# Products of zeros ahead of a conv, and the last tile's products in two halves of the columns

## The chip, the cores and the metric

The kernel runs on one core of one Trainium2 chip. The metric is the device time of one execution in microseconds (us); for the kernel before it is 1641.54 us, the median of three runs (1641.47 to 1641.69).

## The reference, cut to what matters

An input x of 128 sequences, 32 rows each, 512 columns, goes through two blocks, each with a residual:

```python
x = x + attention(conv1d(x) + cond @ c_weight.T + bias)     # grouped conv, 9 taps, 4 groups of 8 rows
x = x + ffn(mix(x, cond))
# mix: att = softmax(gelu(gelu(cond @ W0 + b0) @ W1 + b1) @ W2 + b2); per sequence, a 32x32 matrix
#      att @ weight mixes the 32 rows, and att @ bias_k is added
# ffn: out = x @ base_W.T + low-rank part of the top 2 of 28 experts (rank 8), gated by their softmax
```

The attention has 32 query heads and 8 key heads of 128, with weights given as 4-bit codes and scales.

## The kernel before, in words

The kernel is written engine by engine: each engine has a program of its own, and semaphores (`wait_ge`, `then_inc`) order them. What stands in an engine's program is executed in that order. It has two blocks.

The first block, `prepare_and_convolve`, does the conv, in fp32. SP issues the loads: `params` (which holds cond, W0, W1, W2 and their kin), `band` (the conv taps as a banded matrix), then x in 16 pieces of 512 KB, one for each pair of a 128-column tile k and a group g, in the order in which the conv wants them. TensorE (line 347 on) waits for `params` and runs the small chain that gives the softmax over the 8 matrices: a product into `ctx_psum` for the conv's bias, w0, w1 behind ScalarE's gelu of w0's result, w2 behind the gelu of w1's. VectorE adds the bias and computes the softmax (lines 391 to 403). Behind w2 TensorE goes through the 32 half units of the conv, `conv(n)`: half unit n is 64 of the 128 positions of one unit (k, g), and consists of four products of 160 or 192 columns (line 323) and one or two of 32 columns (lines 328 and 332) that carry the taps over the edge. Results go to banks 0 to 2. VectorE adds the bias into `h_f`, a buffer of two units (`add_ctx`, line 384); `turn(n - 2)` transposes 128x128 pieces of `h_f` on TensorE into banks 3 to 5 (line 344), and ScalarE and VectorE split each into two fp16 parts, high and low, in `hT` (lines 477 and 389). `h_f[:, 1]` is first written by `add_ctx(2)`, and bank 5 by `turn(2)`. An fp32 product shows as two instructions in the profile, and so two of the rows' "x" are one product. The block ends for all engines together when each has finished its program.

The second block, `attention_and_ffn`, goes through 8 key heads and 8 chunks of 512 tokens, with about 90% of the time, and then through 32 tiles of 128 tokens for the mix and the ffn. For a tile t of the steady part, TensorE's order is: `gate_lora(t)` (12 products of 252 columns, line 857: expert logits and low-rank activations of all experts), `mix(t + 1)`, `transpose_acc(t + 3)`, `lora_out(t - 1)` (6 products of 512 columns that close tile t - 1, line 893), `base_out(t)` (12 products of 512 columns into bank 2 or 3, line 872; each accumulation of three passes works on high and low fp16 parts) and `lora_transpose(t)` (line 884), which needs VectorE to have chosen and gated the experts (lines 1162 to 1192). ScalarE and VectorE then take the transposed result out of its bank in two fp16 parts (lines 1508 and 1199), and only then can `lora_out(t)` run. `finish(t)` (line 1206) adds the residual on VectorE and writes `res`, and SP stores it (`store`, line 687), 256 KB for a tile. `y_bank` (bank 0) takes the result of `mix`, and `add_bias` (line 1147) reads it. In the last tile there is no mix and no next tile, so `lora_out(31)` and `finish(31)` follow with nothing beside them.

Of the kernel before, what the change touches and what calls it, by code (L numbers as in the profile page):

```python
# [14 lines left out]
P = 128  # L15
# [140 lines left out]
def prepare_and_convolve(nc, c, a, bank, accT, hT, w, rows):  # L156
# [10 lines left out]
    def sem(name):  # L167
        return c.enter_context(nc.semaphore(name))
# [28 lines left out]
    f_src = sb("f_src", [P, 2, 512])  # L197
    f_hl = sb("f_hl", [P, 2, 2, 512], F16)

    params_loaded = sem("params_loaded")  # L200
    kern_loaded = sem("kern_loaded")
    ident_loaded = sem("ident_loaded")
# [101 lines left out]
    @block.tensor  # L304
    def _(pe):
        def conv(n):

            k, g = unit(n // 2)
            j0 = n % 2 * 4
            if n < 2:  # L310
                pe.wait_ge(band_loaded, 16)
            if n % 2 == 0:
                pe.wait_ge(x_loaded[k][g], 16)
            elif k < KT - 1:
                pe.wait_ge(x_loaded[k + 1][g], 16)
            if n >= 3:
                pe.wait_ge(h_added, n - 2)
            out = bank[n % 3].rearrange("p (s l) -> p s l", s=CG)
            for j in range(4):

                lo, hi = max(LB * j - PAD, 0), min(LB * j - PAD + LT, HALF)
                m0 = lo - (LB * j - PAD)
                pe.matmul(out[:, :, lo:hi], xT[:, k, g, j0 + j], band[:, g, :, m0:m0 + hi - lo], start=j == 0, stop=False,
                          skip_group_check=True)
            mm = None
            if n % 2 or k:
                kk, jj = (k, j0 - 1) if j0 else (k - 1, BLOCKS - 1)
                mm = pe.matmul(out[:, :, 0:PAD], xT[:, kk, g, jj], band[:, g, :, LT - PAD:LT], start=False,
                               stop=n % 2 == 1 and k == KT - 1, skip_group_check=True)
            if n % 2 == 0 or k < KT - 1:  # L330
                kk, jj = (k, j0 + 4) if j0 == 0 else (k + 1, 0)
                mm = pe.matmul(out[:, :, HALF - PAD:HALF], xT[:, kk, g, jj], band[:, g, :, 0:PAD], start=False, stop=True,
                               skip_group_check=True)
            mm.then_inc(conv_psum, 1)

        def turn(t):
            u, half = t // 2, t % 2
            if t == 0:
                pe.wait_ge(ident_loaded, 16)
            pe.wait_ge(h_added, 2 * u + 2)  # L340
            if t >= 3:
                pe.wait_ge(hT_ready, t - 2)
            for s in range(4):
                mm = pe.transpose(bank[3 + t % 3][:, s * P:(s + 1) * P], h_f[:, u % 2, 4 * half + s], w.ident[:])
            mm.then_inc(hT_psum, 1)

        pe.wait_ge(params_loaded, 16)
        pe.matmul(bank[6][:, 0:S], cond_T, cw_T, start=True, stop=True).then_inc(ctx_psum, 1)
        pe.matmul(bank[7][:, 0:B], w0, cond_T, start=True, stop=True).then_inc(hid_psum, 1)
        pe.wait_ge(ctx_added, 1)  # L350
        pe.wait_ge(hid_done, 1)
        pe.matmul(bank[6][:, 0:B], w1, hid[:, 0], start=True, stop=True).then_inc(hid_psum, 1)
        pe.wait_ge(hid_done, 2)
        pe.matmul(bank[7][:, 0:COND_K], hid[:, 1], w2, start=True, stop=True).then_inc(att_psum, 1)
        for n in range(2 * UNITS):
            conv(n)
            if n >= 2:
                turn(n - 2)
            if n == 3:
                pe.wait_ge(att_step, 5)  # L360
                pe.transpose(bank[6][0:COND_K, 0:B], att[:], w.ident[:]).then_inc(att_T_psum, 1)
            if n in (4, 5):
                if n == 4:
                    pe.wait_ge(kern_loaded, 16)
                    pe.wait_ge(att_T_done, 1)
                m = n - 4
                pe.matmul(bank[7 - m], att_T[:], kern[:, 512 * m:512 * (m + 1)], start=True, stop=True).then_inc(agg_psum, 1)
            if n == 6:
                pe.wait_ge(agg_done, 1)
                pe.matmul(bank[7][:, 0:S], att_T[:], kern[:, S * S:], start=True, stop=True).then_inc(agg_psum, 1)  # L370
        turn(2 * UNITS - 2)
        turn(2 * UNITS - 1)

    @block.vector
    def _(dve):
# [59 lines left out]
        def f_lows(m):  # L435
# [3 lines left out]
            dve.scalar_tensor_tensor(out=lo, in0=f_src[parts, m % 2, 0:cols], scalar=FSCALE, in1=hi, op0=ALU.mult,  # L439
                                     op1=ALU.subtract).then_inc(f_low, 1)  # L440

        dve.wait_ge(ctx_psum, 1)
        dve.tensor_tensor(ctx_sb[:], bank[6][:, 0:S], fside, ALU.add).then_inc(ctx_added, 1)
        softmax()
# [54 lines left out]
def attention_and_ffn(nc, c, a, banks, accT, hT, w, rows, out):  # L499
# [144 lines left out]
        return banks[:, 2 + t % 2]  # L644


    def at(step):

        return step[0] * CHUNKS + step[1]
# [16 lines left out]
    def _(sp):  # L666
# [15 lines left out]
        def load_x(t):  # L682
            sp.dma_start(tile_of(t), x_rows[t]).then_inc(x_loaded[t % XTILES], 16)
# [21 lines left out]
        wait_chunk(7)  # L705
        for t in range(XTILES // 2, XTILES):
            load_x(t)
        for t in range(TILES):
            store(t)
            if t + XTILES < TILES:  # L710
                load_x(t + XTILES)
        for n in range(2):
            sp.wait_ge(out_stored[n], 16 * TILES // 2)

    @block.tensor
    def _(pe):
# [116 lines left out]
        def mix(t):  # L833
            if t == 0:
                pe.wait_ge(mixw_loaded, 16 * 2 * TB)
                pe.wait_ge(q_cos_done[0], STEPS)
                pe.wait_ge(q_sin_done[0], STEPS)
            else:
                pe.wait_ge(y_added, t)
            pe.wait_ge(xs_ready, t + 1)  # L840
            for k in range(KT):
                for i, (xp, wp) in enumerate(PASSES):
                    mm = pe.matmul(y_bank[:, k * P:(k + 1) * P], x_hl[:, t % 2, xp, k * P:(k + 1) * P], mixw[:, wp, t],  # L843
                                   start=i == 0, stop=i == 2)
            mm.then_inc(y_psum, 1)
# [16 lines left out]
        def base_out(t):  # L862
            if t >= 2:
                pe.wait_ge(res_done, t - 1)
            else:
                pe.wait_ge(base_loaded, 16)
                pe.wait_ge(q_cos_done[1], STEPS)
                pe.wait_ge(q_sin_done[1], STEPS)
            i = 0
            for k in range(KT):  # L870
                for yp, wp in PASSES:
                    pe.matmul(base_bank(t), y_hl[:, t % 2, yp, k * P:(k + 1) * P], base[:, wp, k],  # L872
                              start=i == 0, stop=False, skip_group_check=True)
                    i += 1

        def lora_transpose(t):
            pe.wait_ge(lora_gated, t + 1)
# [171 lines left out]
        output(LAST, 2, 3)  # L1049
        output(LAST, 3, 3)  # L1050
        lora_transpose(3)
        for t in range(4, TILES):
            gate_lora(t)
            if t + 1 < TILES:
                mix(t + 1)
            if t + 3 < TILES:
                transpose_acc(t + 3)
            lora_out(t - 1)
            base_out(t)
            lora_transpose(t)  # L1060
        lora_out(TILES - 1)


    @block.vector
    def _(dve):
# [239 lines left out]
        for t in range(4, TILES):  # L1305
# [5 lines left out]
                add_x(t + 3)  # L1311
            finish(t - 1)
            lora_low(t)
        finish(TILES - 1)


    @block.gpsimd
# [396 lines left out]
```

## Time and profile before

| what | value |
|---|---|
| median of three runs | 1641.54 us |
| the profiled execution, its own time | 1641.25 us |
| its span | 1639.5 us |
| TensorE busy | 1602.0 us (98%) |
| VectorE, ScalarE, GpSimd busy | 1397.5, 1252.2, 1130.9 us |
| the conv block, to the first product of the next | 79.3 us |
| from the last tile's first gate product to the end of the span | 11.2 us |

The profile is of one execution. Its times are counted from the start of the span. PE is TensorE and PEld its weight loads, DVE is VectorE, ACT ScalarE, POOL GpSimd and SP the engine that issues the DMAs. L323 is line 323 of the kernel. A row of a timeline gives the start, the duration, the engine, the line, the operation, what it writes and reads (partitions x elements), how many instructions are merged in it, and in brackets how long the engine stood idle before it and what ended that. A product's duration includes the way of its last column through the array, so rows that follow one another overlap: the time that one costs is the distance from its start to the next start. Some products of TensorE have a load of their own beside them, which overlaps. A tile of the program can stand under another's name where the two share memory (`codes` holds `res` and `y_f` at the end, `hT` the ffn weights, `w_v` the transposed rank columns, `w_f` the gated ones).

### The profile page before, as it was taken

How to read it: one execution, taken by the hardware profiler on the slowest of the kernel's cores; microseconds unless marked ns; L12 is line 12 of the kernel's file. 1: busy time of each engine (PE TensorE's matmuls, PEld its weight loads, DVE VectorE, ACT ScalarE, POOL GpSimd, SP SyncE). 2: the span in 40 equal slices, each digit the busy share in tenths (PEclk: the TensorE clock that was granted, in tenths of full speed). 3: DMA queues.
4: the chain of work that ended last, by engine and by line, in shares of the span. 5: the costliest groups of instructions: out<-in, count | busy, mean ns of one | idle time of the engine just before them, and what ended most of it. 6: DMA issues, size and time to landing. Idle time of an engine off the chain costs nothing.

```text
span 1639.5 us, 37703 instructions
## 1 busy us (share of the span) xinstructions
PE 1602.0 (98%) x14847; PEld 889.6 (54%) x14848; DVE 1397.5 (85%) x2174; ACT 1252.2 (76%) x2158; POOL 1130.9 (69%) x942
## 2 busy tenths in 40 slices
PE   8979999999999999999999999999999999899998
PEld 8945555555555554555455555555555555566665
DVE  5868888888888888888888888888888888878887
ACT  2468888888888888888888888888888888632222
POOL 1168777877787778777877787778777787633332
PEclk9999999999999999999999999999999999999999
DMA  7400010001000100010001000100000003022221
GB/s 292 130 23 27 14 33 2 27 15 34 1 27 15 34 1 27 15 34 2 27 14 34 1 27 14 34 1 28 15 1 27 25 6 87 27 74 82 78 83 47
DMA packets 32173, 60.83 MB, mean 37 GB/s; under 512 B 11496, under 2 KB 14120, under 8 KB 31744
## 3 DMA queue, kind: packets, MB, share of 16 engines
q1 hardware_dynamic: 32000, 58.42, 11.1%
q8 instruction: 121, 1.98, 0.5%
q14 instruction: 52, 0.43, 0.1%
HBM read 47.46 MB, written 10.95 MB: 36 GB/s over the span
## 4 chain that ended last, share of the span: by engine, by line
PE 66%; DVE 16%; POOL 7%; issue 5%; ACT 1%; DVEq 0%; POOLq 0%
PE banks L816 17%; PE banks L731 16%; PE banks L756 10%; DVE q_sin L1077 8%; PE banks L872 5%; PE banks L745 5%; DVE accT L1140 4%; PE banks L775 4%; PE banks L801 3%; PE banks L893 2%; PE banks L857 2%; DVE pT L1126 2%; POOL q_f L1343 2%; POOL k_f L1328 1%; PE banks L843 1%
## 5 line engine op out<-in xcount | busy, mean ns | idle before, releaser
L731 PE MATMUL banks<-hT,w_q 128*128 128x512 f16 x2048 | 546.7, 379 | 8.9 <-DVE q_sin L1077 5.2
L1466 ACT ACTIVATE banks<-banks,ratios 128x512 f32<-128x512 f32 x768 | 503.4, 664 | 60.8 <-PE banks L731 52.0
L816 PE MATMUL banks<-o_hl,w_o 128*128 128x512 f16 x2048 | 544.1, 380 | 3.5 <-ACT banks L1476 1.7
L1476 ACT ACTIVATE banks<-banks,ratios 128x512 f32<-128x512 f32 x768 | 481.6, 660 | 42.9 <-PE banks L816 40.3
L1343 POOL TENSOR_TENSOR q_f<-q_f,q_sin 128x1024 f32<-128x1024 f32 x128 | 301.4, 2355 | 78.7 <-DVE q_sin L1077 78.7
L816 PEld LDWEIGHTS banks<-o_hl,w_o 128*128 128x128 f16 x2048 | 180.3, 98 | 263.3 <-issue 35.0
L1077 DVE TENSOR_TENSOR q_sin<-banks,rope_q 64x1024 f32<-64x1024 f32 x256 | 312.7, 1222 | 8.2 <-POOL q_f L1343 2.6
L731 PEld LDWEIGHTS banks<-hT,w_q 128*128 128x128 f16 x2048 | 188.8, 98 | 237.7 <-ACT banks L1466 34.2
L756 PE MATMUL banks<-w_v,hT 128*128 128x128 f16 x3072 | 192.9, 219 | 0.0
L1068 DVE TENSOR_SCALAR banks<-banks,ratios 128x512 f32<-128x512 f32 x192 | 145.1, 755 | 53.7 <-PE banks L745 53.7
L756 PEld LDWEIGHTS banks<-w_v,hT 128*128 128x128 f16 x3072 | 177.0, 98 | 21.7
L1077 DVE TENSOR_TENSOR q_f<-banks,rope_q 128x1024 f32<-128x1024 f32 x128 | 155.5, 1215 | 23.4 <-PE banks L731 23.4
L1328 POOL TENSOR_TENSOR k_f<-k_f,rope_k 64x512 f32<-64x512 f32 x128 | 162.6, 1270 | 14.5 <-POOL q_f L1343 10.7
L1140 DVE SCALAR_TENSOR_TENSOR accT<-banks,scales,accT 128x512 f32<-128x512 f32 x224 | 158.0, 746 | 12.5 <-PE banks L816 4.9
L1131 DVE TENSOR_TENSOR o_hl<-banks,o_hl 128x512 f16<-128x512 f32 x256 | 159.1, 683 | 1.9
L1481 ACT ACTIVATE o_hl<-banks 128x512 f16<-128x512 f32 x256 | 132.3, 602 | 26.5 <-PE banks L801 26.2
L745 PE MATMUL banks<-hT,w_k 128*128 128x512 f16 x512 | 152.3, 379 | 0.0
L1347 POOL TENSOR_TENSOR sc<-sc,stats 128x512 f32<-128x512 f32 x64 | 67.0, 1047 | 112.8 <-DVE stats L1111 112.8
L1098 DVE STREAM_TRANSPOSE sc<-banks 128x512 f32<-128x512 f32 x64 | 45.9, 717 | 74.1 <-PE banks L775 74.1
L1412 POOL TENSOR_TENSOR w_q<-hT,w_q 128x512 f16<-128x512 f32 x32 | 37.1, 1159 | 75.7 <-ACT w_q L1496 75.7
L1361 POOL CAST pT_hl<-pT 128x512 f16<-128x512 f32 x64 | 39.0, 610 | 71.3 <-DVE pT L1126 71.3
L872 PE MATMUL banks<-hT,w_o 128*128 128x512 f16 x384 | 88.2, 379 | 0.0
(122 smaller groups left out, 1945.1 us busy)
## 6 DMA issues: line engine op xcount, KB each, us to landing
codes<-in_codes SPq DMA_DIRECT2D x40, 512.0 KB, 3.7
accT<-in_xT SPq DMA_DIRECT2D x16, 512.0 KB, 9.5
hT<-in_x SPq DMA_DIRECT2D x32, 256.0 KB, 2.9
out<-codes SPq DMA_DIRECT2D x32, 256.0 KB, 2.0
v_s<-in_v_scales SPq DMA_DIRECT2D x8, 256.0 KB, 4.5
hT<-aggb_rows SPq DMA_DIRECT2D x1, 2048.0 KB, 7.0
f_src<-in_base_T SPq DMA_DIRECT2D x4, 256.0 KB, 9.3
base_rows<-f_hl SPq DMA_DIRECT2D x4, 256.0 KB, 3.3
```

Of the source, the lines that this page charges most:

```text
L731: mm = pe.matmul(banks[:, tile], w.q[:, n[2], kt * RF * HD + tile * HD:kt * RF * HD + (tile + 1) * HD], hT[:, n[1], kt, hp], start=kt == 0 ...
L745: mm = pe.matmul(kv_bank, w.k[:, n[2], kt * HD:(kt + 1) * HD], hT[:, n[1], kt, hp], start=kt == 0 and hp == 0, stop=hp == 1, skip_group_ch ...
L756: mm = pe.matmul(kv_bank[:, j * HD:(j + 1) * HD], hT[:, n[1], kt, hp, j * P:(j + 1) * P], w.v[:, n[2], wp, kt * HD:(kt + 1) * HD], start=m ...
L816: mm = pe.matmul(o_bank(tile), w.o[:, p[2], h * D + tile * P:h * D + (tile + 1) * P], o_hl[:, op, h], start=h == 0 and op == 0, stop=op == ...
L872: pe.matmul(base_bank(t), y_hl[:, t % 2, yp, k * P:(k + 1) * P], base[:, wp, k], start=i == 0, stop=False, skip_group_check=True)
L1077: return dve.tensor_tensor(dst.rearrange("p t (b s) -> p t b s", s=S), q, t, ALU.mult)
L1131: dve.tensor_tensor(lo, pv_bank(p, b).rearrange("p (j h q) -> p j h q", h=RF, q=S), hi, ALU.subtract).then_inc(out_ready[b], 1)
L1140: ins = dve.scalar_tensor_tensor(out=dst, in0=o_bank(tile), scalar=last, in1=dst, op0=ALU.mult, op1=ALU.add)
L1328: ins = pool.tensor_tensor(by_s(k_f[64 * h:64 * (h + 1), 1]), by_s(k_f[src, 0]), table(w.rope_k[:, n[2], 1], src), ALU.mult)
L1343: pool.tensor_tensor(q, q, q_sin[:], ALU.add).then_inc(q_ready[pair], 1)
L1466: act.activation(banks[:, tile], banks[:, tile], ACT.Copy, scale=w.ratios[:, n[0], tile, kt:kt + 1]).then_inc(q_scaled[tile], 1)
L1476: act.activation(o_bank(tile), o_bank(tile), ACT.Copy, scale=w.ratios[:, p[0], RF + tile, h:h + 1]).then_inc(o_scaled[tile], 1)
```

## The change

On TensorE, a helper `idle_product` multiplies zeros out of `h_f[:, 1]` into bank 5, in fp32. VectorE clears `h_f[:, 1, 0:4]` (512 columns) first. One idle product of 512 columns stands ahead of the wait for `params`; two of 128 columns stand behind the w0 product, two behind w1 and one behind w2. In the second block the last tile leaves the loop: its base products and its low-rank products are done for 256 columns at a time, the first half into bank 3 as before and the second into `y_bank`; nine of the twelve base products of the second half stand ahead of `lora_transpose(31)` and three behind it. VectorE's last sum and SP's last store are cut in two in the same way. `lora_out(30)` keeps its place behind `gate_lora(31)`.

```diff
--- before.py
+++ after.py
@@ -197,6 +197,7 @@
     f_src = sb("f_src", [P, 2, 512])
     f_hl = sb("f_hl", [P, 2, 2, 512], F16)
 
+    zeroed = sem("zeroed")
     params_loaded = sem("params_loaded")
     kern_loaded = sem("kern_loaded")
     ident_loaded = sem("ident_loaded")
@@ -344,14 +345,26 @@
                 mm = pe.transpose(bank[3 + t % 3][:, s * P:(s + 1) * P], h_f[:, u % 2, 4 * half + s], w.ident[:])
             mm.then_inc(hT_psum, 1)
 
+        def idle_product(cols):
+
+            zeros = h_f[:, 1].rearrange("p s l -> p (s l)")
+            pe.matmul(bank[5][:, 0:cols], zeros[:, 0:P], zeros[:, 0:cols], start=True, stop=True)
+
+        pe.wait_ge(zeroed, 1)
+        idle_product(512)
         pe.wait_ge(params_loaded, 16)
         pe.matmul(bank[6][:, 0:S], cond_T, cw_T, start=True, stop=True).then_inc(ctx_psum, 1)
         pe.matmul(bank[7][:, 0:B], w0, cond_T, start=True, stop=True).then_inc(hid_psum, 1)
+        for _ in range(2):
+            idle_product(P)
         pe.wait_ge(ctx_added, 1)
         pe.wait_ge(hid_done, 1)
         pe.matmul(bank[6][:, 0:B], w1, hid[:, 0], start=True, stop=True).then_inc(hid_psum, 1)
+        for _ in range(2):
+            idle_product(P)
         pe.wait_ge(hid_done, 2)
         pe.matmul(bank[7][:, 0:COND_K], hid[:, 1], w2, start=True, stop=True).then_inc(att_psum, 1)
+        idle_product(P)
         for n in range(2 * UNITS):
             conv(n)
             if n >= 2:
@@ -439,6 +452,7 @@
             dve.scalar_tensor_tensor(out=lo, in0=f_src[parts, m % 2, 0:cols], scalar=FSCALE, in1=hi, op0=ALU.mult,
                                      op1=ALU.subtract).then_inc(f_low, 1)
 
+        dve.memset(h_f[:, 1, 0:4], 0.0).then_inc(zeroed, 1)
         dve.wait_ge(ctx_psum, 1)
         dve.tensor_tensor(ctx_sb[:], bank[6][:, 0:S], fside, ALU.add).then_inc(ctx_added, 1)
         softmax()
@@ -644,6 +658,13 @@
         return banks[:, 2 + t % 2]
 
 
+    def half(c):
+        return slice(c * D // 2, (c + 1) * D // 2)
+
+    def end_bank(c):
+
+        return (base_bank(TILES - 1), y_bank)[c][:, 0:D // 2]
+
     def at(step):
 
         return step[0] * CHUNKS + step[1]
@@ -705,12 +726,15 @@
         wait_chunk(7)
         for t in range(XTILES // 2, XTILES):
             load_x(t)
-        for t in range(TILES):
+        for t in range(TILES - 1):
             store(t)
             if t + XTILES < TILES:
                 load_x(t + XTILES)
+        for c in range(2):
+            sp.wait_ge(res_done, TILES + c)
+            sp.dma_start(out_rows[TILES - 1][:, half(c)], res[:, (TILES - 1) % 2, half(c)]).then_inc(out_stored[(TILES - 1) % 2], 16)
         for n in range(2):
-            sp.wait_ge(out_stored[n], 16 * TILES // 2)
+            sp.wait_ge(out_stored[n], 16 * TILES // 2 + 16 * n)
 
     @block.tensor
     def _(pe):
@@ -872,6 +896,28 @@
                     pe.matmul(base_bank(t), y_hl[:, t % 2, yp, k * P:(k + 1) * P], base[:, wp, k],
                               start=i == 0, stop=False, skip_group_check=True)
                     i += 1
+
+        def base_end(c, ks):
+
+            t = TILES - 1
+
+            if c == 0:
+                pe.wait_ge(res_done, t - 1)
+            else:
+                pe.wait_ge(y_added, TILES)
+            for k in ks:
+                for i, (yp, wp) in enumerate(PASSES):
+                    pe.matmul(end_bank(c), y_hl[:, t % 2, yp, k * P:(k + 1) * P], base[:, wp, k, half(c)],
+                              start=k == 0 and i == 0, stop=False, skip_group_check=True)
+
+        def lora_end(c):
+            t = TILES - 1
+            pe.wait_ge(loraT_ready, TILES)
+            for h in range(2):
+                for i, (lp, wp) in enumerate(PASSES):
+                    mm = pe.matmul(end_bank(c), loraT[:, t % 2, lp, h], lb[:, wp, h, half(c)], start=False,
+                                   stop=h == 1 and i == 2, skip_group_check=True)
+            mm.then_inc(ffn_psum, 1)
 
         def lora_transpose(t):
             pe.wait_ge(lora_gated, t + 1)
@@ -1049,16 +1095,22 @@
         output(LAST, 2, 3)
         output(LAST, 3, 3)
         lora_transpose(3)
-        for t in range(4, TILES):
+        for t in range(4, TILES - 1):
             gate_lora(t)
-            if t + 1 < TILES:
-                mix(t + 1)
+            mix(t + 1)
             if t + 3 < TILES:
                 transpose_acc(t + 3)
             lora_out(t - 1)
             base_out(t)
             lora_transpose(t)
-        lora_out(TILES - 1)
+        gate_lora(TILES - 1)
+        lora_out(TILES - 2)
+        base_end(0, range(KT))
+        base_end(1, range(KT - 1))
+        lora_transpose(TILES - 1)
+        base_end(1, (KT - 1,))
+        for c in range(2):
+            lora_end(c)
 
 
     @block.vector
@@ -1311,7 +1363,12 @@
                 add_x(t + 3)
             finish(t - 1)
             lora_low(t)
-        finish(TILES - 1)
+        for c in range(2):
+            t = TILES - 1
+            dve.wait_ge(ffn_psum, TILES + c)
+            dve.wait_ge(out_stored[t % 2], 16 * (t // 2))
+            dve.scalar_tensor_tensor(out=res[:, t % 2, half(c)], in0=end_bank(c), scalar=1 / FSCALE, in1=tile_of(t)[:, half(c)],
+                                     op0=ALU.mult, op1=ALU.add).then_inc(res_done, 1)
 
 
     @block.gpsimd
```

## Rows read from the trace of the kernel before

**Rows 1.** The page: busy time by engine, and one weight load group of it.
```profile
PE 1602.0 (98%) x14847; PEld 889.6 (54%) x14848; DVE 1397.5 (85%) x2174; ACT 1252.2 (76%) x2158; POOL 1130.9 (69%) x942
...
L816 PEld LDWEIGHTS banks<-o_hl,w_o 128*128 128x128 f16 x2048 | 180.3, 98 | 263.3 <-issue 35.0
```

**Rows 2.** Timeline of TensorE, 3 to 19 us: start us, us, engine line op.
```profile
3.41 0.64 PE L348 MATMUL banks<-params 128*128 128x32 f32 x2 [3.41 <-DMA params<-in_params]
...
5.18 0.76 PE L352 MATMUL banks<-hid,params 128*128 128x128 f32 x2 [0.55 <-ACT hid L472]
6.41 0.60 PE L354 MATMUL banks<-params,hid 128*128 128x8 f32 x2 [0.46 <-ACT hid L472]
7.17 2.69 PE L323 MATMUL banks<-band,accT 128*128 128x160 f32 x8 [0.17 <-DMA accT<-in_xT]
...
9.93 2.69 PE L323 MATMUL banks<-band,accT 128*128 128x160 f32 x8
...
13.13 1.56 PE L323 MATMUL banks<-band,accT 128*128 128x160 f32 x8
...
15.15 1.36 PE L323 MATMUL banks<-band,accT 128*128 128x160 f32 x8
...
16.71 0.63 PE L344 MATMUL banks<-ident,h_f 128*128 128x128 f32 x4
...
17.29 1.36 PE L323 MATMUL banks<-band,accT 128*128 128x160 f32 x8
...
18.62 0.64 PE L344 MATMUL banks<-ident,h_f 128*128 128x128 f32 x4
```

**Rows 3.** Timeline of TensorE, the end of the first block.
```profile
76.30 1.32 PE L344 MATMUL banks<-ident,h_f 128*128 128x128 f32 x8 [0.32 <-DVE h_f L384]
79.29 1.02 PE L731 MATMUL banks<-hT,w_q 128*128 128x512 f16 x4 [1.68 <-PEq L75]
```

**Rows 4.** Groups by form, 7.2 to 13.0, then 13.6 to 14.5 us: busy, mean ns.
```profile
L323 PE MATMUL banks<-band,accT 128*128 128x192 f32 x8 | 3.0, 527 | 0.0
...
L323 PE MATMUL banks<-band,accT 128*128 128x192 f32 x4 | 0.8, 326 | 0.0
```

**Rows 5.** Stretches: PE, PEld, DVE, ACT, POOL busy, granted clock, DMA share, GB/s.
```profile
5.00:10.00 5.00, 4.19 (x15) 3.86 (x15) 1.11 (x6) 1.90 (x4) 0.00 (x0) 1.00 0.98 353
10.00:15.00 5.00, 5.00 (x26) 5.00 (x26) 1.51 (x3) 0.00 (x0) 0.00 (x0) 1.00 1.03 395
```

**Rows 6.** Timeline of TensorE, the last tile.
```profile
1628.28 1.46 PE L857 MATMUL banks<-hT,w_o 128*128 128x252 f16 x12
1629.58 1.46 PE L893 MATMUL banks<-hT,w_v 112*128 112x512 f16 x6
1630.87 2.75 PE L872 MATMUL banks<-hT,w_o 128*128 128x512 f16 x12
1633.46 0.38 PE L884 MATMUL banks<-ident,w_f 128*112 128x128 f32 x2
1634.78 1.47 PE L893 MATMUL banks<-hT,w_v 112*128 112x512 f16 x6 [0.93 <-DVE w_v L1199]
```

**Rows 7.** Timelines of VectorE and of ScalarE, the last tile.
```profile
1632.12 0.39 DVE L1192 SCALAR_TENSOR_TENSOR w_f<-banks,gates 128x224 f32<-128x224 f32 x1
...
1634.30 0.42 DVE L1199 TENSOR_TENSOR w_v<-banks,w_v 112x256 f16<-112x256 f32 x1 [1.19 <-ACT w_v L1508]
1636.29 0.69 DVE L1206 SCALAR_TENSOR_TENSOR codes<-banks,hT 128x512 f32<-128x512 f32 x1 [1.56 <-PE banks L893]
...
1633.88 0.38 ACT L1508 ACTIVATE w_v<-banks 112x256 f16<-112x256 f32 x1 [3.26 <-PE banks L884]
```

**Rows 8.** Stretches, behind the last sum, columns as in rows 5.
```profile
1637.00:1639.50 2.50, 0.00 (x0) 0.00 (x0) 0.00 (x0) 0.00 (x0) 0.00 (x0) 0.73 0.28 105
```

**Rows 9.** Stretches, early in the attention block, columns as in rows 5.
```profile
88.00:102.00 14.00, 9.02 (x102) 5.53 (x104) 7.55 (x8) 5.06 (x8) 10.28 (x7) 1.00 0.00 1
102.00:110.00 8.00, 5.40 (x22) 1.45 (x19) 6.64 (x9) 4.17 (x7) 5.52 (x6) 1.00 0.00 0
```

## The prediction

> **What bounds the kernel now.** I read the page first: TensorE is busy 98% of the span [rows 1], so time can come back only where it is slow or waits with nobody else in front of it. The change touches two such places, the first 15 us and the last 11, so I then read the timeline of TensorE at both ends.
>
> At the start the reader is to see two things. First, TensorE idles until params land at 3.41, runs three short products with waits of 0.55 and 0.46 between them, and begins the conv at 7.17, when the first x piece lands [rows 2]. From there the timeline shows it without a wait until 76.3, just before its last turns; the next block starts at 79.29 behind those [rows 3]. So what it gains early it keeps. Second, the clock. The first half-tile (7.17 to 9.93) takes 2.76 us and the second 3.20; the same two shapes later take 1.33 (17.29 to 18.62) and 1.56 (15.15 to 16.71) [rows 2]. A 192-column product falls from 527 to 326 ns [rows 4]. The granted clock reads 1.00 in both stretches [rows 5], so that column holds nothing of this; the durations say that the engine ran at 1.2 GHz until about 13.4 and at 2.4 GHz after it. It rose some 6.2 us after the work became unbroken at 7.17.
>
> At the end the last tile is a chain with nothing beside it: base products 1630.87 to 1633.46, two transposes, ScalarE 0.38, VectorE 0.42, the six last products from 1634.78 (TensorE idle 0.93 before them), the sum on VectorE (0.69 from 1636.29), then the store [rows 6, 7, 8].
>
> **The change at the start.** VectorE, idle here, clears 512 columns of fp32. No row shows a memset of that size; its bounds are nothing and 0.69, which 512 columns with two operands take at the end [rows 7]. I take 0.5, so TensorE starts its 512-column product near 1.4. At the low clock a 128-column fp32 product costs about 0.43 (the two instructions of 5.18 have 0.76 in all with the way out of the array) [rows 2]; four times that is 1.7, so it ends near 3.1, ahead of params at 3.41. It costs nothing: its cover is that DMA, and without cover it is 1.7.
>
> Behind w0 come two 128-column products, 0.85, in front of the w1 product, whose wait ended at 5.18. They start near 4.4 and end near 5.28: w1 late by 0.1. Two more behind w1 make w2 late by another 0.1 to 0.25; one stands behind w2, ending near 7.5 at the low clock, so the conv starts up to 0.35 late, at the low clock worth half that, 0.15, in final time. ScalarE, and the softmax on VectorE behind w2, move by 0.2; they need not be ready before the first conv half is. SP's queue is untouched.
>
> What it may buy is an earlier clock. The products fill the gaps, so that unbroken work begins at 3.41 in place of 7.17. If the clock rises at the same distance behind that, 6.2 us, it rises at about 9.7 in place of 13.4. The work of those 3.7 us then takes half: 1.8, less the 0.15, makes **1.6**. The bounds: nothing (or 0.15 lost) if the clock doesn't move; 3.07 if it is up before 7.17, which is 5.96 less 2.89 for the first two halves [rows 2]. I choose the middle case, because the only rise in the trace needed that long a run of work, and these fillers are short. Is x there in time? DMA moves 353 to 395 GB/s then [rows 5], so a 512 KB piece each 1.3 to 1.5 us: pieces at 7.17, 8.6, 10.0, 11.4, against uses at 7.5, 9.7, 11.8, 13.4 in the middle case and 7.2, 8.5, 10.1, 12.1 in the fastest. It costs 0.1 at worst. Every later load of this block is issued behind semaphores that move along.
>
> A rule of the Trainium skill speaks against trusting this: "TensorE: Matmul & The Clock Gate", Part 1, says that the low clock is the default and activity releases it, but that how many products run at it varies from run to run of one kernel, and that one should not fit a model to a count. By it the start would give anything from 0 to 3.1 and differ between executions. The three runs here lie within 0.22 us, so this kernel's rise seems not to wander by much.
>
> **The change at the end.** The columns of the last tile go in halves to two banks. 24 products of 256 columns replace 12 of 512. 252 columns take 1.30 for 12, 0.108 each, and 512 columns 2.59, 0.216 each [rows 6], so the sum stays 2.59. The change adds a weight load to each pair; one takes 0.098 [rows 1], and if 12 of them showed, 1.2 would be lost, but the 252-column products have a load of that size each and still stand 0.108 apart, which excludes it. The gated rank columns that the transposes read are ready on VectorE at 1632.5 [rows 7], early enough. The transposes move ahead of three half products: 3 x 0.108 = **0.32** earlier, and ScalarE, VectorE and the last products with them; the three run in what was the 0.93 wait. The second half waits for the reader of y_bank, which was done before this tile's gate products could start. The twelve last half products again take 1.30, but the first half's sum runs beside the second's products, and what is left at the end is 256 columns instead of 512: 0.42 by the 256-column subtraction against 0.69 [rows 7], **0.27**. The store: 256 KB keep the 16 DMA engines busy 0.28 x 2.5 = 0.70 us [rows 8]; only 128 KB are left behind the last sum, **0.3** (0 if the fixed part rules, 0.35 if all of it goes). SP issues the first store some 0.6 before the second and one issue takes about 0.35, so they don't meet. Sum at the end: **0.9**, bounds 0.6 and 0.95.
>
> **Sum.** 1.6 + 0.9 = 2.5. The profiled execution took 1641.25 (span 1639.5), 0.3 under the median 1641.54; 2.5 off the median gives **1639.0**. A measurement of this kernel tells about 0.2%, 3.3 us, from no change: the limit lies at 1638.3, so this forecast counts as the same.
>
> **Rivals.**
> 1. *The clock is up before the conv* (chance 0.32). For it: the fillers bring TensorE near unbroken work from 3.41 to 7.17, 3.8 us, and the 512-column product stands before that. Against it: in the trace the conv ran 6.2 us unbroken at the low clock. Gain 3.07 + 0.9 = 4.0: 1637.6, faster by over 0.2%.
> 2. *The zeros don't move the clock* (0.13): the rise depends on what the array really does, or on a moment that the kernel doesn't set. No row shows products of zeros alone, so nothing excludes it. The end alone remains, less 0.15: 1640.8. This is the case in which the change doesn't do what it says.
> 3. *Slower: the clock falls in the thin stretch.* From 88 to 110 TensorE is busy 9.02 of 14 and 5.40 of 8 us [rows 9], and it keeps the high clock. After it stopped at the end it fell: the mean is 0.73 from 1637 to 1639.5 [rows 8]. If the earlier rise, or the shift of the work by 2 to 3 us, lets the clock fall at 88 and stay low to 110, its 14.4 us of work need 28.8 where 22 are there: 6.8 lost, 4.3 net, 1645.8, slower by over 0.2%. It decides from a loss of 2.5 on. That page of the Trainium skill says, under "HAM oscillation", that idle gaps bring the low clock back. Against it: the same gaps were there and it held. Chance 0.04.
> 4. *The rise wanders from execution to execution* (0.06), set by a timer of the chip and not by the engine's work: anything from 1637.6 to 1640.8, its middle near the forecast, a third of it faster by over 0.2%. This is the rule of the Trainium skill cited above. Against it stand the 0.22 us between the three runs, where a rise that wanders by 3 us would give 1.5.
>
> The forecast, with the clock rising while the conv runs (9 to 11), has 0.45.
>
> **How the numbers follow.** The forecast's own range is 1638.4 to 1639.7: the rise an us either way is 0.5, the end 0.4. Rival 1 lies at 1637.4 to 1638.1 and rival 2 at 1640.5 to 1641.2. To hold 8 in 10 the range takes in the forecast, rival 1 and the better part of rival 2: 1637.4 to 1640.8. Faster by over 0.2% is rival 1 and a third of rival 4: 0.34. The same is the forecast, rival 2 and the rest of rival 4: 0.62. Slower: 0.04.
>
> **What would show it.** In the timeline of the changed kernel: a 512-column product that ends before 3.4; the conv's first product between 7.17 and 7.5; the second half tile shared between 192-column products of 527 and of 326 ns, where rival 1 has only those of 326 and rival 2 only those of 527; the start of the attention block moved from 79.29 to about 77.7 (76.2, 79.4 for the rivals). At the end: 256-column products 0.108 apart, 0.32 less from the last gate product to the transposes, a last sum of about 0.42 and about 2.0 from it to the span's end instead of 2.5. Half products 0.16 apart, a wait of TensorE on x, or a granted clock under 1 between 88 and 110 would prove it wrong.

## The result, and the profile after

The changed kernel takes 1638.89 us (median of 20 runs, 1638.17 to 1642.03), the kernel before 1641.8 (20 runs, 1641.47 to 1642.86): a ratio of 0.9985, 95% interval [0.9979, 0.9991] (the medians alone give 0.9982). That is 2.9 us less, within 0.2%, and the forecast was 1639.0. But the profiled execution of the change is not one of the middle: it took 1639.92, and its span is only 1.3 us shorter (1638.1 against 1639.5).

**The start.** The timeline of TensorE in the changed kernel:

```profile
1.45 2.08 PE L351 MATMUL banks<-h_f 128*128 128x512 f32 x2 [1.45 <-DVE h_f L455]
3.32 0.61 PE L356 MATMUL banks<-params 128*128 128x32 f32 x2
...
4.31 1.06 PE L351 MATMUL banks<-h_f 128*128 128x128 f32 x4
5.17 0.67 PE L362 MATMUL banks<-hid,params 128*128 128x128 f32 x2
5.63 1.04 PE L351 MATMUL banks<-h_f 128*128 128x128 f32 x4
6.49 0.31 PE L366 MATMUL banks<-params,hid 128*128 128x8 f32 x2
6.65 0.47 PE L351 MATMUL banks<-h_f 128*128 128x128 f32 x2
7.18 1.43 PE L324 MATMUL banks<-band,accT 128*128 128x160 f32 x8
...
8.66 1.43 PE L324 MATMUL banks<-band,accT 128*128 128x160 f32 x8
...
10.29 1.44 PE L324 MATMUL banks<-band,accT 128*128 128x160 f32 x8
```

The 512-column product begins at 1.45 and is out of the way when params are there, as forecast; from then on the bracket of a wait appears on no row. The clock is where the forecast erred. The product of w2 has 0.31 here against 0.60 [rows 2]: the engine is at 2.4 GHz from about 6.4 on. The conv begins at 7.18, its first half takes 1.48 and the second 1.63. This is rival 1. The attention block begins at 76.33 in place of 79.29 [rows 3], 2.96 earlier:

```profile
76.33 1.02 PE L755 MATMUL banks<-hT,w_q 128*128 128x512 f16 x4 [1.68 <-PEq L75]
```

From here on, the *lead* is by how much an instruction starts earlier than the same one in the first profile of the kernel before.

**The middle** gives back more than half of that. Here is the change at the last round of the attention:

```profile
1403.83 0.63 PE L854 MATMUL banks<-ident,accT 128*128 128x128 f32 x4 [0.78 <-ACT v_f L1549]
1405.46 1.41 PE L840 MATMUL banks<-o_hl,w_o 128*128 128x512 f16 x4 [1.00 <-DVE o_hl L1183]
```

and the same two places of the kernel before:

```profile
1405.62 0.63 PE L830 MATMUL banks<-ident,accT 128*128 128x128 f32 x4 [0.78 <-ACT v_f L1492]
1407.25 1.04 PE L816 MATMUL banks<-o_hl,w_o 128*128 128x512 f16 x4 [1.00 <-DVE o_hl L1131]
```

1403.83 against 1405.62: the lead is 1.79 there, no longer 2.96, and by the last tile's first gate product it is 0.48 (1627.80 against 1628.28 in [rows 6]). Part of the reason is in the granted clock of two stretches of the change (columns as in [rows 5]; the granted clock is the third number from the end):

```profile
108.80:112.20 3.40, 3.40 (x38) 2.85 (x27) 2.22 (x2) 2.14 (x5) 3.17 (x3) 0.52 0.02 5
1406.00:1409.00 3.00, 3.00 (x11) 1.30 (x8) 1.28 (x2) 2.22 (x4) 2.79 (x3) 0.50 0.47 154
```

Near half in both: the clock stood at 1.2 GHz, from 108.9 and again from 1406.0 on. The text calls this a fall of the clock. The first cost 0.3 of the lead, the second 1.3. Where it fell the engine had just been thin, as the waits of 0.78 and 1.00 above show; but the kernel before has the same two waits, and in this profile no fall behind them, so a thin place alone doesn't bring one.

**The end**, TensorE and then VectorE:

```profile
1627.80 1.46 PE L881 MATMUL banks<-hT,w_o 128*128 128x252 f16 x12
...
1632.69 0.38 PE L930 MATMUL banks<-ident,w_f 128*112 128x128 f32 x2
1632.91 0.49 PE L910 MATMUL banks<-hT,w_o 128*128 128x256 f16 x3
1634.01 1.48 PE L918 MATMUL banks<-hT,w_v 112*128 112x256 f16 x12 [0.61 <-DVE w_v L1251]
```

```profile
1633.52 0.42 DVE L1251 TENSOR_TENSOR w_v<-banks,w_v 112x256 f16<-112x256 f32 x1 [0.89 <-ACT w_v L1565]
1634.87 0.42 DVE L1370 SCALAR_TENSOR_TENSOR codes<-banks,hT 128x256 f32<-128x256 f32 x1 [0.92 <-PE banks L918]
1635.53 0.42 DVE L1370 SCALAR_TENSOR_TENSOR codes<-banks,hT 128x256 f32<-128x256 f32 x1 [0.23 <-PE banks L918]
```

From the first gate product to the transposes 4.89 us pass in place of 5.18, the wait before the last products is 0.61 in place of 0.93, the last sum takes 0.42 in place of 0.69 [rows 6, 7], and from its end to the end of the span it is 2.18 (1635.95 to 1638.13) against 2.48. Together 10.33 in place of 11.18 from the first gate product on: 0.85.

So this execution's sum is: 2.96 won at the start, 2.48 lost on the way (to a lead of 0.48: 1.6 by the two falls, 0.7 by two steps that are looked into below, and 0.15 bit by bit between 125 and 890 us), 0.85 won at the end, 1.33 in all.

### The profile page after: what moved, and what is told of

Same layout as the page of the kernel before. It is cut to its first block, busy times and chain, and to the rows that moved or that the text cites. A ratio compares the mean times of both kernels' runs of the same rounds, so it can differ in the third digit from the quotient of the medians.

```text
span 1638.1 us, 37768 instructions
## 1 busy us (share of the span) xinstructions
PE 1605.0 (98%) x14878; PEld 892.8 (54%) x14878; DVE 1399.9 (85%) x2176; ACT 1252.8 (76%) x2158; POOL 1132.7 (69%) x942
## 4 chain that ended last, share of the span: by engine, by line
PE 66%; DVE 16%; POOL 6%; issue 5%; ACT 1%; DVEq 0%; POOLq 0%
PE banks L840 17%; PE banks L755 16%; PE banks L780 10%; DVE q_sin L1129 9%; PE banks L769 5%; PE banks L896 5%; DVE accT L1192 4%; PE banks L799 4%; PE banks L825 3%; DVE pT L1178 2%; PE banks L939 2%; PE banks L881 2%; POOL q_f L1400 2%; PE banks L867 1%; POOL k_f L1385 1%
## 5 line engine op out<-in xcount | busy, mean ns | idle before, releaser
L1385 POOL TENSOR_TENSOR k_f<-k_f,rope_k 64x512 f32<-64x512 f32 x128 | 162.7, 1271 | 14.5 <-POOL q_f L1400 10.7
```

The source lines that it names most:

```text
L1385: ins = pool.tensor_tensor(by_s(k_f[64 * h:64 * (h + 1), 1]), by_s(k_f[src, 0]), table(w.rope_k[:, n[2], 1], src), ALU.mult)
```

## The experiments

Two theories stood after this. Mine: the start is worth 3 us in full, and about 1 is given back in the attention block, by a clock that falls where TensorE is thin, and by something that isn't the clock. The rival: the fillers bring less than 3 in most executions, and the profile showed a favourable start. The times below are medians of 11 runs, each beside 33 runs of the kernel before on the same chip.

### Start alone, end alone

e1 keeps the new first block and takes the old second one; e2 the other way round.

> The idle products alone, the end as before. Theory (the clock is up before the conv, 3 us are won there, and about 1 is given back later on by a clock that falls in the attention block): the first conv half lasts about 1.5 us, the attention block begins at 76.3 in place of 79.3, and the time is 1.5 to 2.4 us under that of before. Rival (the start is worth its full 3.0 in most runs, and it is the end that brings less than its 0.9): 2.9 to 3.1 under.

> The halves of the last tile alone, the start as before. Theory: 0.6 to 0.95 us under the time of before, all of it behind the last base product (transposes 0.33 earlier, last sum 0.27 shorter, store about 0.25 shorter). Rival (the end brings nothing that a measurement shows): within 0.3 of before.

e1 took 1639.53 against 1641.46, 1.9 under (ratio 0.999 [0.9981, 0.9999]). The number is the one that my theory gave, but its reason isn't: the profiled execution (1639.53) begins the attention block at 76.84, not 76.3, and shows no granted clock under 1 before its last 1.6 us. What it gives back are the two steps alone: 2.45 less 0.7 is 1.7, which is what its span is shorter by. Its 11 runs lie in two groups, six at 1639.24 to 1639.53 and five at 1640.49 to 1640.81, about 1.3 apart, the price of the second fall; the upper five have a mean granted clock of 0.998 or 0.997, the lower six 0.999, but no upper one was profiled. e2 took 1640.68, 0.8 under; its interval [0.9985, 1.0004] does not exclude no change, but its profile shows the end at 10.33 us again, as in the change. 0.8 and 1.9 make 2.7, beside 2.9 for the whole. That fits two parts which simply add, but each interval is about 3 us wide, and so the sum is no proof of it.

e2 has the old start, and yet it begins otherwise than the kernel before:

```profile
7.21 2.68 PE L323 MATMUL banks<-band,accT 128*128 128x160 f32 x8
...
9.97 1.96 PE L323 MATMUL banks<-band,accT 128*128 128x160 f32 x8
...
12.13 1.44 PE L323 MATMUL banks<-band,accT 128*128 128x160 f32 x8
```

The second conv half costs 2.16 (9.97 to 12.13) and not 3.20 [rows 2]: its clock rose near 11, not near 13.4, with the same program for TensorE up to there. So the moment of the rise is not the kernel's alone. The attention block begins at 78.17, a lead of 1.12, without any product of zeros.

And the clock falls in e2 too, three times, at 89.6, 110.0 and 1407.1. Two of these stretches:

```profile
110.10:113.40 3.30, 3.30 (x68) 3.10 (x61) 2.01 (x3) 2.59 (x5) 3.07 (x3) 0.50 0.02 5
1407.20:1410.50 3.30, 3.30 (x14) 1.44 (x16) 1.05 (x2) 2.42 (x5) 2.88 (x3) 0.50 0.43 138
```

The first fall costs nothing that lasts, the second 0.2, the third 1.3, and the lead of 1.12 is a lag of 0.5 at the last tile. The falls are therefore not the change's own. Each execution, profiled or not, has a mean granted clock on record. In the profiles, 0.998 goes with two such falls, 0.997 with three, and 0.999 or 1.000 with none. Of the 66 executions of the kernel before that ran beside e1 to e8, 51 have 0.998 or 0.997; both of its profiles have 1.000, and so show its rarer kind. A lead or a loss that is told against them is told against an execution without falls. The two kinds take the same time (medians of 1641.48 with 0.998 or less, 1641.38 with 1.000). e2 shows one way to that, an earlier rise that the falls eat up, but of the kernel before itself no such execution was profiled.

### Which of the products does it

e3 takes out the 512-column product and keeps the five fillers:

```diff
-        idle_product(512)
```

e4 takes out all five fillers and keeps that product; the first two of them:

```diff
-        for _ in range(2):
-            idle_product(P)
...
```

> The change without the 512-column product ahead of params; the five fillers of 128 columns stay. Theory A (the fillers raise the clock, and the first product does nothing for it): 192-column products of the first conv half at 326 ns and the attention block at 76.3, as with all of them. Theory B (the rise needs the run of work that begins at 1.45): the clock rises while the conv runs, as was forecast, at 9 to 10, the second half mixes 527 and 326 ns, and the attention block begins at 77.6 to 78.

> The change with the 512-column product alone, no fillers. Theory A (the fillers do it): the clock rises near 13.4 as before, the first two conv halves take 2.8 and 3.2 us and the attention block begins at 79.3; time 0.9 under before. Theory B (an early start of work is what counts): the rise comes at 10 or earlier, and the block begins at 77.7 or earlier.

e4: its conv ran at the low clock until about 11.3 and the block began at 78.14, as in e2 (78.17), which has no idle product at all: the first product alone brings nothing to the start. The time, 1641.69 against 1641.46 (ratio 1.0004 [0.9995, 1.0013]), missed its expectation of 0.9 under. Two steps of the kind looked into next take 0.7 of the 0.85 that the end brings, and the rest is within the noise.

e3: 1641.79, ratio 0.9997 [0.9988, 1.0006], though the profiled execution is one of its three best (1638.57) and has the block's begin at 76.70. For the start Theory A holds here, and in two more profiles without the early product further down, e7 (rise at 7.9) and e11 (6.7); a third, e12 (9.2), comes nearer Theory B. In all four profiles without the fillers the rise is at 11.0 or later. So it is the fillers that bring the early rise. The time is another matter: the other eight runs of e3 lie at 1640.04 to 1642.64, while 14 of the change's 20 lie below 1639.2, and e11 (1640.05) shows that such a run can have the full early start and lose it later. In their lowest group are 5 of 22 runs of e3 and e7, which lack the early product, 14 of 20 of the change and 5 of 11 of e5. These counts favour the early product, but e5 and e7, the one pair measured side by side, have 5 and 2 of 11, too few to tell them apart, and how a product that ends near 3.5 us could keep the clock up later is not shown.

### What takes 0.7 us in the attention block

Beside the falls, the lead shrank twice by 0.35, near 895 and near 980 us, in every profile of a kernel with the memset on VectorE. VectorE around the first of them, in the kernel before and in the change:

```profile
895.84 0.25 DVE L1119 RECIPROCAL stats<-stats 128x16 f32<-128x16 f32 x1
896.48 1.22 DVE L1077 TENSOR_TENSOR q_f<-banks,rope_q 128x1024 f32<-128x1024 f32 x1 [0.38 <-PE banks L731]
```

```profile
893.31 0.25 DVE L1171 RECIPROCAL stats<-stats 128x16 f32<-128x16 f32 x1
894.30 1.23 DVE L1129 TENSOR_TENSOR q_f<-banks,rope_q 128x1024 f32<-128x1024 f32 x1 [0.74 <-PE banks L755]
```

The same product of q begins 0.64 behind the reciprocal before and 0.99 behind it after; the wait in front has grown from 0.38 to 0.74. e5 gives the clearing to GpSimd:

```diff
-        dve.memset(h_f[:, 1, 0:4], 0.0).then_inc(zeroed, 1)
+        pool.memset(h_f[:, 1, 0:4], 0.0).then_inc(zeroed, 1)
```

> The change with the clearing of h_f on GpSimd in place of VectorE, so that VectorE's program has one instruction less. Theory A (the two steps of 0.35 us near 895 and 980 us, which every kernel with the memset on VectorE shows against the one before and the kernel without it doesn't, come from VectorE's instructions standing one place later): the steps are gone, the attention block runs at the pace of before, and the median is 0.7 under that of the change, 3.4 to 3.7 under before. Theory B (they come from the added products on TensorE): the steps stay and the median is 2.7 to 3.0 under before.

```profile
893.33 0.25 DVE L1171 RECIPROCAL stats<-stats 128x16 f32<-128x16 f32 x1
893.96 1.23 DVE L1129 TENSOR_TENSOR q_f<-banks,rope_q 128x1024 f32<-128x1024 f32 x1 [0.38 <-PE banks L755]
```

0.63 behind the reciprocal, a wait of 0.38: the step is gone, and so is the second. All that differs for VectorE is that the memset is gone and each of its other instructions stands one place earlier in its program. The steps are in all seven profiles of kernels with that memset on VectorE (the change, e1, e3, e4, e10, e11, e12), and in none of those without it there (before, e2, e9, and e5 to e8, which have it on GpSimd). What in the engine makes the place matter was not tried, nor another instruction in the memset's stead.

But GpSimd now has one instruction more, and it shows the same thing, which the expectation didn't foresee. Near 1400 us, first the change, then e5 with GpSimd and VectorE:

```profile
1397.97 2.36 POOL L1400 TENSOR_TENSOR q_f<-q_f,q_sin 128x1024 f32<-128x1024 f32 x1 [0.72 <-DVE q_sin L1129]
```

```profile
1397.55 2.36 POOL L1400 TENSOR_TENSOR q_f<-q_f,q_sin 128x1024 f32<-128x1024 f32 x1 [1.00 <-DVE q_sin L1129]
1399.95 2.46 DVE L1129 TENSOR_TENSOR q_sin<-banks,rope_q 64x1024 f32<-64x1024 f32 x2 [0.26 <-POOL q_f L1400]
```

GpSimd's product comes 0.28 later behind the same VectorE product, VectorE waits 0.26 for it, and the lead shrinks by 0.23. This step is in all four profiles with the clearing on GpSimd (e5 to e8) and in none of the other ten. So the move wins 0.7 and costs 0.2, about 0.5 in all.

The median did not follow the expectation: 1639.39 against 1641.47 (0.9983 [0.9974, 0.9992]), 2.1 under where 3.4 to 3.7 were expected. The profiled execution (1639.42) had falls at 87.8, 108.3 and 1405.3. The other five runs of its upper half were not profiled; four of them have a mean granted clock of 0.998 or 0.997 too, one has 0.999. The five lowest lie at 1637.85 to 1638.09, about 0.8 under the bulk of the change's runs (1638.5 to 1639.1), but the kernel before was 0.3 faster on this occasion (1641.47 against 1641.8), which leaves 0.5, as the steps say.

### Keeping the clock up

e6 is e5 with 14 products added in the two waits near 1404, each of 256 columns of w.k into bank 0, which is free there. e8 is e6 and also (second diff) fills the wait of 1.68 before the attention block. e7 is e5 without the 512-column product.

```diff
         project_v(LAST, 1)
+        idle_mm(6)
         transpose_acc(0)
+        idle_mm(8)
         output(PRIOR, 0, 0)
```

```diff
         turn(2 * UNITS - 1)
+        for _ in range(5):
+            pe.matmul(bank[6][:, 0:P], w.ident[:], w.ident[:], start=True, stop=True)
```

> As e5, and 14 products of 256 columns into bank 0 fill the two gaps of TensorE at the step from the attention to its last round (near 1402 to 1405 us, waits of 0.78 and 1.00). Theory (in some executions the clock falls there and costs 1.3; filled gaps keep it up): no execution with a fall near 1406, a spread of runs without the group 1.3 above the fastest, and the median at the fastest group, 3.5 to 4.0 under before. Rival (the products only lengthen the chain): 0.1 to 0.5 slower than e5 in its fastest runs.

> As e5 without the 512-column product. In e3, the same with the memset on VectorE, 3 of 11 runs lay near 1638.6 and 8 at 1640.0 to 1642.6. Theory A (without the early product the rise of the clock comes in some executions before the conv and in others well inside it): the profile shows a rise between 6 and 11 us, runs spread again over 3 us or more, and the fastest lie 0.7 under those of e3. Theory B (the spread of e3 comes from falls later on and the start is always the same): the attention block begins at 76.3 to 76.9 again, in the profile of a run of the upper group too.

> As e6, and five 128-column fp32 products behind the last turn of the conv, in the wait of 1.68 us before the attention block. Theory (a fall of the clock at the change of block is what puts some runs 3 us higher): no run over 1 us above the fastest group. Rival (those runs come from elsewhere): the group 3 us above the fastest stays as frequent as in the change, 3 in 20.

e6: 1638.05 against 1641.47, ratio 0.9982 [0.9973, 0.9991]; eight runs at 1637.61 to 1638.30, three at 1639.88 to 1640.98, where none was expected 1.3 above the lowest. The median is 3.4 under, where 3.5 to 4.0 were expected. The fillers stand in the gaps without lengthening the chain: behind them the lead is 2.14, of 2.36, and in e7, without them, 2.19 of 2.42.

```profile
1402.32 0.82 PE L1035 MATMUL banks<-w_k 128*128 128x256 f16 x6
1403.26 0.63 PE L854 MATMUL banks<-ident,accT 128*128 128x128 f32 x4
1403.72 1.04 PE L1035 MATMUL banks<-w_k 128*128 128x256 f16 x8
1405.11 1.04 PE L840 MATMUL banks<-o_hl,w_o 128*128 128x512 f16 x4 [0.35 <-DVE o_hl L1189]
```

e8: 1638.03, 0.9981 [0.9972, 0.999]; ten runs at 1637.78 to 1638.69 and one at 1640.28. Its wait before the attention block is 0.56 in place of 1.68, and the block begins as early as in e5 (76.53):

```profile
74.70 1.28 PE L387 MATMUL banks<-ident 128*128 128x128 f32 x10
76.54 1.02 PE L757 MATMUL banks<-hT,w_q 128*128 128x512 f16 x4 [0.56 <-PEq L75]
```

That is 3.4 us under the kernel before, where the change has 2.9; the two were not run side by side, and one against the other they are the same within what can be told. The gain seems to lie in the spread: one run in 11 stands over 1 us above its lowest, and three in e6, against six in 20 for the change and six in 11 for e5. e8's expectation was none, and one in 11 is no clear step down from 3 in 20. Executions with a mean granted clock of 0.998 or less were 14 of 20 in the change, 5 of 11 in e5, 4 in e6 and 3 in e8. So the fillers may keep the clock up, but it isn't shown: the profiles of e6 and e8 have no fall, and neither has that of e7 without them, and none of the upper runs was profiled.

e7: 1640.03, only two of 11 runs under 1639, and its profiled one of them (1638.19). The rise is at 7.9 and the block begins at 76.86, which both of its theories allow; the one about an upper run was not tested.

### The same kernels once more

Four single executions, one each for e9 to e12, to see what changes when nothing in the kernel does.

> The kernel before, a second execution profiled. Theory (the moment of the rise isn't set by the kernel alone): the rise is at another moment than 13.4, between 10 and 13.4, and the attention block begins 0.3 to 1.7 us before 79.3. Rival (it is always at 13.4 here): 527 ns products to 13.4 and the block at 79.3 again.

> The change, a second execution profiled. Theory: the rise lies between 5 and 8 us and the block begins at 76.3 to 76.9; the steps of 0.35 near 895 and 980 are there again; whether the clock falls near 1406 is open. Rival: the same moments as in the first profile, with the falls at 108.8 and 1405.9.

> The kernel of e3, a second execution profiled; 8 of its 11 runs lay at 1640.0 to 1642.6, so that this one is likely to be of them. Theory (without the early product the rise comes in many executions well inside the conv): the first conv halves at 527 ns and the block at 77.5 or later, with a fall near 1406 on top. Rival (the start is the same, all comes from falls later): the block at 76.3 to 76.9, and two or more falls after it that cost 1.3 or more each.

> The same, a third execution, with the same two expectations.

e9 went against my theory: the kernel before had its rise near 13.3 and the block at 79.23 again, and its mean granted clock is 1.000 again, so that it too is of the rarer kind. Two old starts at 13.3 to 13.4 stand beside e2's at 11.0, and the kernel before has runs from 1640.4 to 1642.6; the moment moves, but how often was not settled.

e10, the change again (1638.97, in its bulk): no granted clock under 1 in its whole span,

```profile
1406.00:1409.00 3.00, 2.85 (x32) 1.49 (x34) 1.67 (x3) 2.51 (x5) 3.00 (x3) 1.00 0.63 214
```

the two steps of 0.35 again, and the block at 77.18, later than expected, a lead of only 2.11. This time the first piece of x was late (landed at 7.92, in the first profile at 7.04), with the clock already up:

```profile
6.92 0.66 PE L351 MATMUL banks<-h_f 128*128 128x128 f32 x2
8.06 1.43 PE L324 MATMUL banks<-band,accT 128*128 128x160 f32 x8 [0.47 <-DMA accT<-in_xT]
```

2.11 less 0.7 plus 0.85 is 2.3, which is what its span is shorter by (1637.2 against 1639.5).

e11 (1640.05): block at 76.59, a fall at 109.2 that cost 0.3 and one at 1406.3 that cost 1.4. That is the rival's picture: the start is as good as ever, and the loss comes later. e12 (1642.48) shows how a run comes to the uppermost group, and lies between the two expectations. The rise comes inside the first conv half, near 9.2:

```profile
7.50 2.20 PE L324 MATMUL banks<-band,accT 128*128 128x160 f32 x8
...
9.68 1.44 PE L324 MATMUL banks<-band,accT 128*128 128x160 f32 x8
```

and the clock falls at 77.5, just when the attention block has begun (77.35), so that its first products run at half speed:

```profile
77.50:80.90 3.40, 3.40 (x9) 1.21 (x8) 0.76 (x1) 1.35 (x3) 0.00 (x0) 0.50 0.70 190
```

It had two more falls, near 111.6 and 1408.7. Its lead went from 1.94 at the block to about 0.25 behind that first fall, 1.7 lost, and to a lag of 2.1 behind the last. Three falls (1.7, 0.3 and 1.3) and the two steps (0.7) ate more than the gain of the start.

## Why the prediction was right, and where it wasn't

The time came out as forecast, 1638.89 against 1639.0, but the closeness is in part luck. Two steps were wrong and partly cancelled: the start brings more than it was given, and the middle gives back what was put at nothing. And the kernel before took 1641.8 beside the change, 0.3 more than the 1641.54 that the forecast was taken from: 2.5 less was forecast, 2.9 came.

- *The first product costs nothing; the chain behind w0, w1 and w2 moves by 0.1 to 0.2, the conv starts between 7.17 and 7.5.* Right for the first profile, 7.18, and for e12, 7.50 at the low clock, as the bound said. Other profiles with the fillers have 7.6 (e1) to 8.06 (e10).
- *x is there in time, it costs 0.1 at worst.* Wrong for e10: its first piece landed 0.9 later than in the first profile, TensorE waited for it, and the lead was 0.85 less. The moment of 7.17 came from one trace; in the 14 profiles the piece lands between 6.4 and 7.9.
- *The clock rises 6.2 us behind the begin of unbroken work, at 9.7, worth 1.6.* Wrong. Nine of the ten profiles with the fillers have the rise at 5.9 to 8.0 us, worth 2.96 in the first profile and 2.1 to 2.8 in the others; only e12, at 9.2 and worth 1.94, comes near the forecast. I took one distance from one trace, 6.2, for a property of the chip; in e2, with the same start, it was 3.8. The term was too small by 1.4 in the first profile and by 0.5 in e10. This is rival 1, though in e1, e3 and e7 the rise fell just inside the conv.
- *The rise seems not to wander, as three runs lie within 0.22 us.* Wrong, and rival 4 had half of it: with the start of the kernel before the rise stood at 11.0 (e2), 13.3 (e9) and 13.4, and 33 runs of the kernel before spread over 2.2 us, where the first three had spread over 0.22. But the engine's work counts as well: with the fillers no rise came later than 9.2, without them none before 11.0. The rule of the Trainium skill ("TensorE: Matmul & The Clock Gate", Part 1), that the number of products at the low clock varies from run to run of one kernel, agrees with these traces.
- *The falling clock costs 4 to 7 us in the thin stretch and hardly happens* (rival 3). Half right in the place, wrong in size and frequency. The clock falls in many executions and, by their mean granted clocks, in most of the kernel before. A fall near 89 cost nothing that lasts and one near 109 cost 0.2 to 0.3, one near 1406 cost 1.3 to 1.4 and the one at the change of block 1.7. The latter two lie at waits of TensorE that the trace of before already has. The prediction named a granted clock under 1 between 88 and 110 as a sign against it; the first profile has one from 108.9 on, and it didn't decide the time. The reason for the small chance, that the same gaps were there and the clock held, was one trace, and that trace is of the rarer kind.
- *Nothing else is touched.* Wrong by 0.7: one instruction more on VectorE, costed at nothing because the engine is idle at that time, delayed VectorE in two places 900 us later.
- *Zeros might not count* (rival 2): they count, in that multiplying zeros was enough: the rise came at 5.9 to 9.2 with the five fillers (ten profiles) and at 11.0 to 13.4 without (four).
- *The end: 0.32 + 0.27 + 0.3 = 0.9.* Right: 0.29 + 0.26 + 0.30 = 0.85. Products of 256 columns stand 0.109 apart. From the last sum to the span's end the prediction looks for about 2.0, but its own term of 0.3 makes that 2.2, and 2.18 came.

In sum, against an execution of the kernel before without falls: 2.1 to 3.0 at the start, 0.7 lost to VectorE's program, 0 (e10) or 1.6 (first profile) lost to falls, 0.85 at the end. For e10 that is 2.3, and 3.1 at most. The three runs of the change near 1642 are 2.1 above the profiled one; what they lost was not profiled.

## What to carry to other kernels

Products of zeros in the gaps ahead of a dense stretch can lift TensorE's clock before or just as it begins; where they stand in a wait they cost nothing. Filling later thin places may keep the clock up, which these runs don't settle. Judge such a change by the spread of many runs and by more than one profile, of the kernel before too: one profile here had a block's begin 0.9 us from that of another execution of the same kernel, and both profiles of the kernel before were of its rarer kind. An added instruction can cost time far from where it stands, on either of the engines tried here, so compare both traces at landmarks far behind the edit, not only around it.

## What the runs showed of the hardware

One instruction more at the head of VectorE's program made it 0.35 us late near 895 us and again near 980 us, in all seven profiles that have it there. Moving it to GpSimd removed both and made a GpSimd product 0.28 late near 1398 us, in all four profiles. Falls of the clock to 1.2 GHz come in some executions of a kernel and not in others, among them behind waits of 0.78 and 1.00 us (cost 1.3) and of 1.68 us (cost 1.7, e12). With the same program at the start the clock rose at 11.0, 13.3 and 13.4 us. Two executions of the same kernel had their first x piece 0.9 us apart (7.04 and 7.92).
